# First expert stage writes its tiles to pair order by indirect writes, and the second attention loads them by plain transfers

## The chip, the core and the metric

The kernel runs on one core of a Trainium2 chip, as one launch. The time is the device time of that core in microseconds, the median over executions. The core's engines are PE (TensorE), DVE (VectorE), ACT (ScalarE), POOL (GpSimd) and SP (SyncE); PEld is PE's load of stationary operands. They run their own instruction streams and meet at semaphores.

## The reference

A decoder of four layers over x, 32 sequences of 128 rows with 128 columns, float32. Each layer adds a cross attention to a context of the same shape, then a mixture of experts with 8 experts. Rows are normed ahead of each.

```python
x = x + xattn0(ctx, norm(x));  x = x + ffn0(norm(x))   # each row goes to 2 of 8 experts (gelu, 512 wide)
x = x + xattn1(norm(x), ctx);  x = x + ffn1(norm(x))   # 2 of 8, gated, at most 256 slots an expert
x = x + xattn2(ctx, norm(x));  x = x + ffn2(norm(x))   # 2 of 8, gated
x = x + xattn3(norm(x), ctx);  x = x + ffn3(norm(x))   # 1 of 8 (gelu)
# ffn with two choices: out[row] = w0[row] * expert[e0[row]](row) + w1[row] * expert[e1[row]](row)
```

xattn1 is a linear attention with 16 heads of 8 columns: softmax over the columns of a head for queries and keys, keys times values summed over the context, queries times that sum, and a projection.

## The kernel before

The 4096 rows stay in SBUF as `x_rows`, 32 tiles of 128 rows, worked on in groups of four tiles. A stage ends with a barrier of all engines. The stages stand in this order: attention 0, router 0, experts 0, attention 1, router 1, experts 1, attention 2, experts 2, attention 3, experts 3, combine and store. Layers are counted from 0, so that "first expert stage" is `experts(0)` and "second attention" is `attention_1`.

**Router.** `route(layer, top, capacity)` sorts the (row, choice) pairs by expert. A slot is a place in that order, and a tile is 128 slots of one expert; layer 0 has 71 tiles (`TILES_TOP2`), layer 1 has 16. PE turns "which slot has this row" into "which row stands in this slot" by matmuls of one-hot halves: eight batches (`eight`), each of eight matmuls (line 1012) for layer 0, each after DVE has made its operands (lines 842 to 844) in one of two buffers. DVE then writes `source_rows` (line 921). For a layer in the list `SCATTERED`, eight more matmuls a batch (line 1016) mark whether the slot holds a pair and which choice, and DVE makes `pair_rows` of them (lines 923 to 932): for each slot the place of its pair, or a spare row of its own for an empty slot. For a layer not in it, DVE keeps `slots` instead (line 890): for each pair the slot it went to.

**Experts.** For each tile, in order: POOL gathers its 128 rows from `normed_rows_dram` by one indirect transfer (line 1152, 64 KB, buffer j modulo 8); PE turns it (line 1173); DVE copies the turned tile and the tile's expert weights into place (1255, 1257); PE multiplies (1183), ACT applies gelu (1217), PE multiplies again (1195), and DVE adds the bias (1249, semaphore `expert_kept`). PE's step k does turn k+2, first product k+1, second product k. For a layer outside `SCATTERED`, SP stores the tile in slot order (line 1136). For one in it, POOL writes the rows by an indirect transfer at `pair_rows` (line 1157), in the same loop and queue as the gathers: at step j it gathers tile j and then writes tile j - LAG, with LAG = 6. The gather of tile j waits only until PE has turned tile j - 8.

```python
for j in range(n_tiles + LAG):
    if j < n_tiles and not kept:
        if j >= SLOTS:
            pool.wait_ge(rows_turned.sem, ...)
        pool.indirect_dma_start(xr[:, j % SLOTS, :], None, xn, ...)
    i = j - LAG
    if scatters and i >= 0:
        pool.wait_ge(expert_kept.sem, ...)
        pool.indirect_dma_start(ys, ..., yo[:, i % SLOTS, :], None)
```

Layers 2 and 3 also write by line 1157, but there SP loads the tiles, so that POOL issues one indirect transfer a tile. Layer 1 issues both.

**Second attention.** It begins with a phase on the context alone: for each of eight groups PE projects keys and values (1550, 1569), DVE subtracts the maximum (1433, 1434), ACT exponentiates (1538), DVE scales (1448 to 1450), PE sums (1576) and DVE masks (1456, 1458). Between these, DVE adds the experts' rows to `x_rows`, weighted (`combine`, line 496), for groups 0 to 3 and takes their statistics; groups 4 to 7 follow in the second turn of the query phase. In the kernel before, POOL gathers those rows by 64 indirect transfers (line 1293, `gather_turns`), one for each tile and choice, and tells DVE by `rows_here`. The fourth attention (after layer 2) instead loads them by eight transfers of SP (`load_pairs`, line 1314, 512 KB each), since layer 2 writes in pair order. The code of DVE is written out by hand in its order; nothing is scheduled.

Of the kernel before, what the change touches and what calls it, by code (L numbers as in the profile page):

```python
# [31 lines left out]
MASKED = -1e30  # L32
FAR = 1.0e6
CAPACITY = 256
SCATTERED = (1, 2, 3)
KEPT = (2, 3)
REGION = B * P + P
SLOTS = 8
# [74 lines left out]
def build(nc, A, out):  # L113
    with ExitStack() as top:
# [147 lines left out]
        def flat(ap):  # L262
            return ap.rearrange("p a d -> p (a d)")
# [13 lines left out]
        with ExitStack() as ph:  # L277
            block = ph.enter_context(nc.Block())
# [193 lines left out]
        def combine_stream(dve, ch, i, w, layer):  # L472

            if layer in SCATTERED:
                dve.wait_ge(pairs_here[w].sem, i * 16 + (pairs_here[w].value + 16))
# [12 lines left out]
        def combine(dve, ch, g, layer):  # L488

            slots = CHOICES[layer]  # L490
            for k in range(slots):
                for j in range(G):
                    t = g * G + j
                    xt = flat(X[:, bass.ds(t, 1), :])
                    row = YY[:, bass.ds(t, 1), k, :] if layer in SCATTERED and slots == 2 else (XN, Y1)[k][:, bass.ds(t, 1), :]
                    ins = dve.scalar_tensor_tensor(xt, flat(row), WT[:, k, bass.ds(t, 1)], xt, ALU.mult, ALU.add)  # L496
# [276 lines left out]
        def route(layer, top, capacity):  # L773

            n_tiles = {0: TILES_TOP2, 1: TILES_CAP, 2: TILES_TOP2, 3: TILES_TOP1}[layer]
            with ExitStack() as ph:
# [56 lines left out]
                def _(dve):  # L833
# [48 lines left out]
                    if capacity:  # L882

                        ch.link(dve.tensor_tensor(posf[:, :, :], posf[:, :, :], keep[:, :, :], ALU.mult))
                        if layer not in SCATTERED:
                            dve.tensor_copy(POS[:, :, :], posf[:, :, :])
                        ch.link(dve.tensor_scalar(tmp[:, 0:2 * B // E, :].rearrange("p a e -> p (a e)"), keep[:, :, :].rearrange("p a b -> p (a b)"), -FAR, FAR, ALU.mult, ALU.add))
                        ch.link(dve.tensor_tensor(posf[:, :, :].rearrange("p a b -> p (a b)"), posf[:, :, :].rearrange("p a b -> p (a b)"), tmp[:, 0:2 * B // E, :].rearrange("p a e -> p (a e)"), ALU.add))
                    elif layer not in SCATTERED:
                        dve.tensor_copy(POS[:, 0:top, :], posf[:, 0:top, :])  # L890
# [30 lines left out]
                    dve.tensor_scalar(SOURCE[:, 0:n_tiles], found, float(HALF), None, ALU.add)  # L921
                    if layer in SCATTERED:
                        ch.link(dve.tensor_copy(pair_used[:, :], first))
# [44 lines left out]
                def _(pe):  # L968
# [39 lines left out]
                    def eight(i, s, first):  # L1008
                        pe.wait_ge(tiles_marked.sem, i + (marked0 + 1))
                        for r in range(EIGHT):  # L1010
                            own = bank[7][:, 0:n_tiles]
                            ins = pe.matmul(own, hot_row[:, s, :, r], row_at_tile[:, s, :, r], start=first and s == 0 and r == 0, stop=True, skip_group_check=True)
                            if layer in SCATTERED:
                                k = r % top
# [273 lines left out]
        def gather_group(pool, g, top):  # L1288

            for t in range(g * G, (g + 1) * G):  # L1290
                for k in range(top):
                    dst = (XN, Y1)[k]
                    pool.indirect_dma_start(dst[:, t, :], None, ys[0:TILES_TOP2 * P, :], bass.IndirectOffsetOnAxis(ap=POS[:, k, t:t + 1], axis=0)).then_inc(gathered[g % 2].sem, 16)

        def group_is_here(pool, g, top):
            pool.wait_ge(gathered[g % 2].sem, gathered[g % 2].value + 16 * G * top * (g // 2 + 1))
            pool.sem_inc(rows_here.sem, 1)
# [6 lines left out]
        def load_pairs(sp, layer):  # L1304

            top = CHOICES[layer]
            dst = YY if top == 2 else XN
            src = ys[0:top * B * P, :].rearrange("(t p k) d -> p t k d", p=P, k=2) if top == 2 else ys[0:B * P, :].rearrange("(t p) d -> p t d", p=P)
            for i in range(TURNS):
                for w in range(W):  # L1310
                    if i:
                        sp.wait_ge(pairs_here[w].sem, pairs_here[w].value + 16 * i)
                    at = slice((i * W + w) * G, (i * W + w + 1) * G)
                    sp.dma_start(dst[:, at], src[:, at]).then_inc(pairs_here[w].sem, 16)
# [58 lines left out]
        def gather_turns(pool, layer):  # L1373

            top = CHOICES[layer]
            for g in range(NG + 1):
                if g < NG:
                    gather_group(pool, g, top)
                if g >= 1:
                    group_is_here(pool, g - 1, top)  # L1380


        def attention_1(layer_before):
            assert layer_before not in SCATTERED
            with ExitStack() as ph:
                VX, KX = P + 16, P + 32
                FIRST = streams(pe=["kv_in", "kv"], act=["ctx_kept", "k_exp"], dve=["k_less", "v_scaled", "kv_masked"], tail=False)
# [16 lines left out]
                block = ph.enter_context(nc.Block())  # L1404
# [1 line left out]
                def first(g):  # L1406
                    return g // W, FIRST[g % W], T[g % W]

                @block.gpsimd
                def _(pool):  # L1410
                    gather_turns(pool, layer_before)

                @block.sync
                def _(sp):
                    sp.wait_ge(SS[W - 1].dve.sem, SS[W - 1].DVE.at(TURNS - 1, "u_normed"))
                    sp.dma_start(head_raw[:, 0:INNER], A["L2_xattn_Wq"]).then_inc(weights_x.sem, 16)
                    sp.dma_start(head_raw[:, INNER:3 * INNER], A["L2_xattn_Wkv"]).then_inc(weights_x.sem, 16)
                    sp.dma_start(head_o.rearrange("p (c d) -> p c d", d=P), A["L2_xattn_Wo"].rearrange("(c p) d -> p c d", p=P)).then_inc(weights_x.sem, 16)
# [966 lines left out]
        route(0, 2, 0)  # L2385
        experts(0)
        attention_1(0)
        route(1, 2, CAPACITY)
        experts(1)
# [26 lines left out]
```

## Time and profile before

| | us |
|---|---|
| median of 3 runs (1900.53 to 1907.52) | 1901.37 |
| the profiled execution's own time | 1909.33 |
| its span, first to last instruction | 1907.6 |
| PE busy | 1488.1 (78%) |
| DVE busy | 1164.3 (61%) |
| ACT busy | 824.9 (43%) |
| POOL busy | 763.8 (40%) |
| mean granted TensorE clock | 0.852 |

The shares are means over stages with different limits, so the stage is what is read: experts 0 from 186 to 341 us, the second attention from 343.6 to 596, experts 1 from 623.9 to 676. A wait in the profile is named by what ended it; "remote" means that the semaphore rose just then, but that no instruction of the profile ended near that moment, and "issue" that nothing shown was waited for.

### The profile page before, as it was taken

What the parts mean: (1) busy time and instruction counts of PE and PEld (TensorE: products, weight loads), DVE (VectorE), ACT (ScalarE), POOL (GpSimd) and SP (SyncE); (2) the same over time, 40 slices, a digit from 0 to 9 for tenths busy, and PEclk for the clock granted to TensorE, in tenths of its full rate; (3) what the DMA queues carried; (4) which work ended last, traced back from release to release, by engine and by line L of the source; (5) the groups of instructions that cost most, each with busy time, mean ns of one, the idle gap of its engine ahead of it and who ended that gap; (6) DMA issues with size and microseconds to landing.
All of it is one profiled execution on the core that took longest, in us unless ns stands there. A gap on an engine that the chain in (4) does not pass through costs nothing. (4 is left out here: it accounts for less than half of the span.)

```text
span 1907.6 us, 36653 instructions
## 1 busy us (share of the span) xinstructions
PE 1488.1 (78%) x10440; PEld 1337.0 (70%) x10441; DVE 1164.3 (61%) x3672; ACT 824.9 (43%) x2537; POOL 763.8 (40%) x757
## 2 busy tenths in 40 slices
PE   6776999425677639999999999999994898446394
PEld 4555899313466539999999999999993787224294
DVE  4556344217867337787778777777775455574244
ACT  4343455201222126666666666666661232313152
POOL 2011543560000535454747474756454355011442
PEclk8786899756666769999999999999997899766597
DMA  9002322110011230000000000000001522200223
GB/s 190 1 0 70 118 65 59 47 48 1 1 45 45 57 97 13 1 12 1 24 1 22 0 22 1 21 0 11 3 10 34 149 72 65 89 9 14 63 64 114
DMA packets 91845, 79.06 MB, mean 41 GB/s; under 512 B 16820, under 2 KB 78871, under 8 KB 91623
## 3 DMA queue, kind: packets, MB, share of 16 engines
q1 hardware_dynamic: 70712, 44.92, 9.0%
q0 software_dynamic: 11936, 24.52, 4.4%
q10 hardware_dynamic: 9104, 8.53, 1.5%
q8 instruction: 41, 0.67, 0.1%
q14 instruction: 52, 0.43, 0.1%
HBM read 51.36 MB, written 27.60 MB: 41 GB/s over the span
## 5 line engine op out<-in xcount | busy, mean ns | idle before, releaser
L1838 POOL TENSOR_TENSOR paired_rows<-paired_rows,rinv 128x1024 f32<-128x1024 f32 x128 | 242.3, 1893 | 284.6 <-DVE rinv L2123 281.6
L2002 ACT ACTIVATE paired_rows<-psum_banks,neg_max 128x256 f32<-128x256 f32 x512 | 237.4, 490 | 0.2
L2114 DVE TENSOR_TENSOR probs_turned_lo<-psum_banks,probs_turned_hi 128x512 fp32r<-128x512 f32 x256 | 175.5, 686 | 96.4 <-ACT probs_turned_hi L1984 82.8
L1888 PE MATMUL psum_banks<-y_turned_parts,queries_hi 128*128 128x256 f32 x1024 | 199.9, 293 | 3.0 <-DVEq L1739 3.0
L1923 PE MATMUL psum_banks<-probs_turned_hi,y_rows 128*128 128x512 f32 x512 | 192.0, 416 | 0.4 <-issue 0.4
L1984 ACT CAST probs_turned_hi<-psum_banks 128x512 fp32r<-128x512 f32 x256 | 151.1, 590 | 57.5 <-PE psum_banks L1872 55.1
L1872 PE MATMUL psum_banks<-ident,paired_rows 128*128 128x128 f32 x1024 | 154.9, 274 | 7.8 <-DVEq L1739 4.4
L1888 PEld LDWEIGHTS psum_banks<-y_turned_parts,queries_hi 128*128 128x128 f32 x1024 | 158.0, 191 | 3.5 <-issue 3.5
L2128 DVE TENSOR_REDUCE neg_max<-psum_banks 128x4 f32<-128x1024 f32 x128 | 155.9, 1218 | 6.5 <-PE psum_banks L1888 3.5
L1984 ACT CAST queries_hi<-psum_banks 128x512 fp32r<-128x512 f32 x128 | 75.0, 586 | 172.5 <-PE psum_banks L1911 167.6
L1888 PE MATMUL psum_banks<-y_turned_parts,queries_lo 128*128 128x256 f32 x512 | 144.5, 282 | 0.0
L1935 PEld LDWEIGHTS psum_banks<-expert_w_a,paired_rows 128*128 128x128 f32 x1024 | 133.8, 191 | 11.2 <-DVE paired_rows L2138 0.8
L1911 PE MATMUL psum_banks<-expert_w_b,expert_w_a 128*128 (+1 forms) x1024 | 138.6, 279 | 3.5 <-ACT tail_turned L1974 1.8
L1935 PE MATMUL psum_banks<-expert_w_a,paired_rows 128*128 128x128 f32 x1024 | 134.7, 274 | 0.6 <-issue 0.6
L1911 PEld LDWEIGHTS psum_banks<-expert_w_b,expert_w_a 128*128 128x128 f32 x1024 | 126.2, 193 | 7.4 <-ACT tail_turned L1974 3.2
L1872 PEld LDWEIGHTS psum_banks<-ident,paired_rows 128*128 128x128 f32 x1024 | 119.6, 142 | 10.6 <-DVEq L1739 5.1
L2114 DVE TENSOR_TENSOR queries_lo<-psum_banks,queries_hi 128x512 fp32r<-128x512 f32 x128 | 88.4, 690 | 43.6 <-ACT queries_hi L1984 34.8
L2002 ACT ACTIVATION_READ_ACCUMULATOR paired_rows<-psum_banks,neg_max 128x1 f32 x512 | 113.6, 222 | 0.0
L1217 ACT ACTIVATE hidden<-psum_banks,tile_w 128x128 f32<-128x128 f32 x284 | 81.2, 368 | 71.7 <-PE psum_banks L1183 52.1
L1923 PEld LDWEIGHTS psum_banks<-probs_turned_hi,y_rows 128*128 128x128 f32 x512 | 96.3, 188 | 17.9 <-issue 0.5
L1152 POOL DMA_INDIRECT tile_rows<-normed_rows_dram,source_rows x71 | 67.3, 948 | 93.5 <-PE psum_banks L1173 65.4
L1923 PE MATMUL psum_banks<-probs_turned_lo,y_rows 128*128 128x512 f32 x256 | 100.2, 391 | 0.0
(717 smaller groups left out, 3386.2 us busy)
## 6 DMA issues: line engine op xcount, KB each, us to landing
tile_rows__<-rows_by_expert SPq DMA_DIRECT2D x71, 64.5 KB
expert_rows<-expert_rows_sb SPq DMA_DIRECT2D x71, 64.0 KB, 1.5
normed_rows_dram<-paired_rows SPq DMA_DIRECT2D x2, 2048.0 KB, 8.9
staged_pairs<-expert_rows SPq DMA_DIRECT2D x8, 512.0 KB
paired_rows<-expert_rows SPq DMA_DIRECT2D x8, 512.0 KB, 6.0
tile_rows___<-rows_by_expert SPq DMA_DIRECT2D x39, 64.5 KB
x_rows<-in_x_dram SPq DMA_DIRECT2D x8, 256.0 KB, 5.3
expert_w_b<-in_L_ffn_w_dram SPq DMA_DIRECT2D x1, 2048.0 KB
```

What stands on the lines that cost most here:

```text
L1152: pool.indirect_dma_start(xr[:, j % SLOTS, :], None, xn, bass.IndirectOffsetOnAxis(ap=SOURCE[:, j:j + 1], axis=0)).then_inc(sorted_in[j % ...
L1217: ins = act.activation(hidT[:, s % 2, c * P:(c + 1) * P], hidden_bank(s, c // 2)[:, c % 2 * P:(c % 2 + 1) * P], ACT.Gelu, bias=w1[:, s % 4 ...
L1838: ins = pool.tensor_tensor(probs[:, p, :, :], probs[:, p, :, :], rinv[:, p, :].unsqueeze(2).to_broadcast([P, 4, 256]), ALU.mult)
L1872: ins = pe.transpose(bank[T_BANK][:, h * P:(h + 1) * P], probs[:, par, h, c * P:(c + 1) * P], ident[:, :])
L1888: ins = pe.matmul(bank[S_BANKS[par] + h // 2][:, (h % 2) * 256:(h % 2 + 1) * 256], queries[q][:, h, :], yparts[:, 2 * s2 + y, :], start=(k ...
L1911: ins = pe.matmul(bank[Q_BANK][:, h * P:(h + 1) * P], wqk[:, 4 * u3 + h, :], flat(KVT[:, bass.ds(b3, 1), P:2 * P]), start=True, stop=True)
L1923: ins = pe.matmul(bank[Z_BANK][:, :], yrows[:, 2 * s1 + y, k * P:(k + 1) * P], probsT[p][:, (u + 1) % 2, k, :], start=(k == 0 and n == 0), ...
L1935: ins = pe.matmul(bank[Y_BANK][:, 0:P], mixed[:, par, h, :], wvo[:, 4 * u0 + h, :], start=(u0 == 0 and h == 0), stop=(u0 == 3 and h == 3), ...
L1984: ins = act.copy(dst, bank[bank_][:, :])
L2002: ins = act.activation(probs[:, par, h, :], bank[S_BANKS[par] + h // 2][:, (h % 2) * 256:(h % 2 + 1) * 256], ACT.Exp, bias=nmax[:, par, h: ...
L2114: ins = dve.tensor_tensor(lo, bank[bank_][:, :], hi.bitcast(F32), ALU.subtract)
L2128: ins = dve.tensor_reduce(nmax[:, par, :], ps[:, S_BANKS[par]:S_BANKS[par] + 2, :].rearrange("p r (h k) -> p (r h) k", k=256), AX.X, ALU.m ...
```

## The change

Layer 0 joins `SCATTERED`, and the second attention takes its rows by `load_pairs`:

```diff
-SCATTERED = (1, 2, 3)
+SCATTERED = (0, 1, 2, 3)
...
         def attention_1(layer_before):
-            assert layer_before not in SCATTERED
+            assert layer_before in SCATTERED
...
-                @block.gpsimd
-                def _(pool):
-                    gather_turns(pool, layer_before)
-
                 @block.sync
                 def _(sp):
+                    load_pairs(sp, layer_before)
                     sp.wait_ge(SS[W - 1].dve.sem, SS[W - 1].DVE.at(TURNS - 1, "u_normed"))
```

Four things follow from the first line. Router 0 gets line 1016 on PE and lines 923 to 932 on DVE, and loses line 890. In experts 0, POOL writes tiles by line 1157, and SP's 71 stores go. DVE's combine of layer 0 reads both choices of a row side by side. Arithmetic is unchanged.

On PE in router 0, each batch of eight matmuls becomes one of sixteen; before the change and after it a batch begins so:

```order
-L1012 MATMUL psum_banks<-row_at_tile,hot_slot_row 128x71 x16
+L1012 MATMUL psum_banks<-row_at_tile,hot_slot_row 128x71
+L1016 MATMUL psum_banks<-hot_tile,hot_slot_row 128x71
+L1012 MATMUL psum_banks<-row_at_tile,hot_slot_row 128x71
+L1016 MATMUL psum_banks<-hot_tile,hot_slot_row 128x71
```

The second kind stands between the first ones, with a weight load of its own each.

On POOL, from experts 0 into the second attention (`expert_kept` is DVE's line 1249, `rows_turned` is PE's line 1173):

```order
-L1152 DMA tile_rows<-normed_rows_dram,source_rows 128x128 x8
-L1152 DMA tile_rows<-normed_rows_dram,source_rows 128x128 [waits rows_turned] x63
-L1047 UNCONDITIONAL_BRANCH
-L1409 UNCONDITIONAL_BRANCH [waits barrier_Pool_Activation_PE_DVE_SP_gather]
-L1293 DMA paired_rows<-expert_rows,slots 128x128 x16
...
+L1152 DMA tile_rows<-normed_rows_dram,source_rows 128x128 x7
+L1157 DMA expert_rows<-expert_rows_sb,pair_rows 17280x128 [waits expert_kept]
+L1152 DMA tile_rows<-normed_rows_dram,source_rows 128x128
+L1157 DMA expert_rows<-expert_rows_sb,pair_rows 17280x128 [waits expert_kept]
+L1152 DMA tile_rows<-normed_rows_dram,source_rows 128x128 [waits rows_turned]
```

From the eighth gather on, each gather stands behind a write that waits for a finished tile, seven tiles back; seven writes follow the last gather. The 64 gathers of line 1293 are gone.

On SP the stores go and the loads come (the rows between are the same pair for tile after tile):

```order
-L1136 ISA [waits expert_kept]
-L1136 DMA expert_rows<-expert_rows_sb 128x128
...
+L1314 DMA paired_rows<-expert_rows 128x4x256 x4
+L1314 DMA paired_rows<-expert_rows 128x4x256 [waits pairs_here0]
+L1314 DMA paired_rows<-expert_rows 128x4x256 [waits pairs_here1]
+L1314 DMA paired_rows<-expert_rows 128x4x256 [waits pairs_here2]
+L1314 DMA paired_rows<-expert_rows 128x4x256 [waits pairs_here3]
```

The first four loads stand at the head of the second attention with no wait; each later one waits only for the landing of its forerunner.

## Rows read from the trace of the kernel before

**Rows 1.** Waits, 200 to 341 us (us in total, times, longest).

```profile
POOL tile_rows L1152 <- PE psum_banks L1173: 65.4, 60, 1.9
```

**Rows 2.** Instructions of lines 1152 and 1173 (ns min/median/max, first and last start).

```profile
L1152 POOL DMA_INDIRECT tile_rows<-normed_rows_dram,source_rows x71: 938/942/1209, 186.0 to 320.8; - x71
...
L1173 PE MATMUL psum_banks<-ident,tile_rows x71: 272/273/477, 193.3 to 335.8; 128*128 128x128 f32 x71
```

**Rows 3.** Timeline, first expert stage and its end: start, length, instruction, [idle before].

```profile
201.35 0.29 DVE L1249 TENSOR_TENSOR expert_rows_sb<-psum_banks,expert_b 128x128 f32<-128x128 f32 x1 [3.77 <-PE psum_banks L1195]
...
341.03 0.29 DVE L1249 TENSOR_TENSOR expert_rows_sb<-psum_banks,expert_b 128x128 f32<-128x128 f32 x1 [0.96 <-PE psum_banks L1195]
...
343.63 0.62 ACT L1527 COPY u_rows<-ctx_turned 128x512 f32<-128x512 f32 x1 [4.16 <-PEq L1047]
```

**Rows 4.** Timeline, second expert stage: POOL's reads and writes in turn, and two rows of PE.

```profile
638.34 1.01 POOL L1157 DMA_INDIRECT expert_rows<-expert_rows_sb_,pair_rows  x1 [5.96 <-ACT expert_rows_sb_ L1223]
...
642.23 0.96 POOL L1152 DMA_INDIRECT tile_rows_<-normed_rows_dram,source_rows  x1 [0.30 <-PE psum_banks L1173]
...
645.15 0.27 PE L1173 MATMUL psum_banks<-ident,tile_rows_ 128*128 128x128 f32 x1
...
653.42 0.98 POOL L1157 DMA_INDIRECT expert_rows<-expert_rows_sb_,pair_rows  x1 [2.54 <-ACT expert_rows_sb_ L1223]
...
664.14 0.98 POOL L1157 DMA_INDIRECT expert_rows<-expert_rows_sb_,pair_rows  x1 [0.76 <-issue]
```

**Rows 5.** Timeline, second expert stage: a late release, then its last write and the next stage.

```profile
645.85 1.16 PE L1183 MATMUL psum_banks<-tile_turned_,expert_w_b 128*128 128x128 f32 x8 [0.43 <-issue]
...
649.81 0.42 DVE L1262 TENSOR_TENSOR hidden_<-psum_banks,gate_ 128x256 f32<-128x256 f32 x1 [4.01 <-remote]
...
675.87 0.96 POOL L1157 DMA_INDIRECT expert_rows<-expert_rows_sb_,pair_rows  x1 [0.31 <-issue]
...
681.29 0.38 SPq L1704 DMA_DIRECT2D staged_pairs<-expert_rows  x1
```

**Rows 6.** Instructions of line 1293, then the timeline of the second attention's start.

```profile
L1293 POOL DMA_INDIRECT paired_rows<-expert_rows,slots x64: 940/944/953, 344.3 to 423.0; - x64
...
345.26 3.78 PE L1569 MATMUL psum_banks<-wsmall,u_rows 128*128 128x256 f32 x8
...
360.80 1.14 PE L1576 MATMUL psum_banks<-expert_w_a 128*128 128x144 f32 x8
...
397.67 0.69 DVE L1433 TENSOR_REDUCE head_sums___<-psum_banks 128x64 f32<-128x512 f32 x1 [37.12 <-remote]
...
420.06 0.61 DVE L1456 TENSOR_TENSOR expert_w_a<-psum_banks,head_blocks 128x432 f32<-128x432 f32 x1 [16.25 <-remote]
...
433.36 0.61 DVE L1456 TENSOR_TENSOR expert_w_a<-psum_banks,head_blocks 128x432 f32<-128x432 f32 x1 [12.48 <-remote]
...
467.42 1.12 DVE L450 TENSOR_SCALAR u_rows<-x_rows,mean_var__,rstd__ 128x128 f32<-128x128 f32 x4
```

**Rows 7.** Transfers (KB each, median us to landing).

```profile
paired_rows<-expert_rows SPq DMA_DIRECT2D x8, 512.0 KB, 6.0
```

**Rows 8.** Fourth attention: instructions of line 2257 and a wait of DVE.

```profile
L2257 POOL DMA_INDIRECT rows_by_expert<-paired_rows,top_experts x32: 965/969/1009, 1708.7 to 1788.0; - x32
...
1729.76 0.69 DVE L2336 TENSOR_REDUCE neg_max<-psum_banks 128x4 f32<-128x512 f32 x1 [13.07 <-remote]
```

**Rows 9.** Timeline, first router: the last batch of eight on PE, DVE's line 921 after it.

```profile
182.04 1.26 PE L1012 MATMUL psum_banks<-row_at_tile,hot_slot_row 128*128 128x71 f16 x8 [0.31 <-DVE row_at_tile L844]
...
184.77 0.23 DVE L921 TENSOR_SCALAR source_rows<-psum_banks 128x71 uint32<-128x71 f32 x1
```

**Rows 10.** Timeline, second router: first and last of DVE's eight steps on pairs.

```profile
621.45 0.16 DVE L923 COPY pair_used_<-psum_banks 128x16 f32<-128x16 f32 x1
...
622.85 0.17 DVE L932 TENSOR_TENSOR pair_rows<-pair_found_,pair_spare_ 128x16 uint32<-128x16 f32 x1
```

**Rows 11.** Instructions of line 1257 (ns min/median/max, first and last start).

```profile
L1257 DVE COPY tile_w<-expert_w_a x71: 417/419/491, 194.1 to 337.0; 128x516 f32 x71
```

## The prediction

> **What bounds the kernel now.** I read the waits of each stage first, then the timeline where one stage hands over to the next, then every place where POOL issues indirect transfers. The page's table alone misleads: PE is 78% busy as a mean, but the change touches two stages that lie apart. In the first expert stage PE is the bound. POOL's 71 gathers wait for PE's turns, 65.4 us in 60 waits [rows 1], and PE turns 71 tiles from 193.3 to 335.8 us, 2.04 us a tile [rows 2]. In the second attention nothing is busy. POOL issues 64 gathers from 344.3 to 424 us, one each 1.25 us (the last starts at 423.0, so 78.7/63), and DVE stands still three times, 37.12, 16.25 and 12.48 us, released by "remote" [rows 6]. The middle of these waits is the strangest: the reader should see that the matmuls which the releases belong to (line 1569 and, from 360.80, line 1576) stand in the timeline as started before 362 us, while DVE's waiting instructions start at 397.67 and 420.06. So PE's release comes up to 58 us after its matmuls as recorded.
>
> That late release has company. In the fourth attention POOL issues 16 indirect writes from 1708.7 us, and DVE waits 13.07 us for a "remote" release [rows 8]. In the second expert stage, POOL's gathers and writes alternate without a gap, PE's line 1183 is recorded at 645.85 for 1.16 us, and DVE's instruction behind it starts at 649.81 [rows 5]. All these stand inside or just behind 10 or more indirect transfers in a row. I take it that a dense row of POOL's transfers holds PE's releases back; the trace does not say how.
>
> **The change part by part.** All differences are taken in the profiled execution (1909.33 us, 8.0 us over the median of the runs shown) and added to the median, 1901.37.
>
> *Router 0.* PE gets 64 matmuls more. A batch of eight takes 1.26 us, so one follows another each 0.136 us if the last takes 0.31, an estimate [rows 9]. Sixteen need 2.2 us, and with a hand-over about 2.25. Then PE sets the pace instead of DVE: eight batches take 18.0 us instead of 12.6 (from 170.7 to 182.04 + 1.26), 5.4 us later. DVE's line 921 starts at 184.77 [rows 9], 1.5 us after PE's last batch, because it has other work first; that hides 1.2, and 4.2 stay. DVE's eight steps more cost 1.6 us, from 621.45 to 623.02 in the second router [rows 10]; the dropped line 890 is one short cast, counted as 0. Sum +5.8. The low end is 1.6, where PE keeps up at its upper clock level.
>
> *Experts 0.* POOL's row becomes gather, write, gather, write. One indirect gather costs 0.942 us [rows 2] and a write 0.98 to 1.01, with 0.30 between; a pair in the second expert stage is 2.57 us (638.34 to 640.91 by that sum). PE needs 2.04 a tile, so POOL becomes the bound. Write 0 needs tile 0, whose bias add starts at 201.35 and takes 0.29 [rows 3]: write 0 starts at 201.9. From it to write 64, the first behind the last gather, stand 64 pairs. Then come six more writes at 1.28 us, 7.7 us; tile 70's gather, 1.3 us ahead of write 64, lands in 2.9 (642.23 to 645.15 [rows 4], line 1173 after line 1152) and needs 5.5 from turn to bias add (335.8 to 341.3 [rows 2, 3]), which is 7.1 and fits. From the issue of the last write to the next stage are 5.4 us in the second expert stage (675.87 to 681.29 [rows 5]) and I take 5.8. So the second attention starts at 201.9 + 64p + 13.5 instead of 343.6 [rows 3].
>
> The size of p decides. Its lower end is 2.57, a POOL that never waits: +36.3 us. The nearest row that has everything is the second expert stage: write 0 at 638.34 and write 9 at 664.14 are nine pairs apart, 2.87 us a pair, since POOL waited 2.54 us once for tiles that PE's late release had delayed [rows 4]. That gives +55.5. Layer 0 is heavier, 2.04 us a tile on PE, against 12 matmuls where it has 16, and PE's clock falls after a wait of some us, so each late release costs more. I take p = 2.95: 64 x 2.95 = 188.8, the next stage at 404.2, +60.6. The upper end: a wait of 3.5 us each 15 us and another 2.5 us at the lower clock leave 9 us of work in 15, 4.6 tiles, p = 3.25, +79.8. SP's 71 stores and DVE's waits for them are gone; SP was not waited for, so that is worth nothing but the 2.3 us of the last landing, which is in the difference above.
>
> What is queued behind the new wait: gather j stands behind write j-7. PE's second product of tile k stands behind the turn of tile k+2, so tile k is finished about 5.6 us after gather k+2 was issued (2.9 to land, 2.7 of work, an estimate), and its write comes six and a half pairs, 16.7 us, after gather k; gather k+2 is two pairs, 5.1 us, behind gather k. That leaves 16.7 - 5.1 - 2.9 - 2.7 = 6 us in which PE may be late without POOL noticing. Beyond it POOL waits, and PE's loads come later by as much.
>
> *Second attention.* 64 gathers go from POOL. SP issues four loads of 512 KB at once, 6.0 us to landing each in the fourth attention [rows 7]; the first is wanted 24 us after the stage's start even without the stalls (434 - 65.9 - 343.6), so they are hidden. If the three stalls go, 37.12 + 16.25 + 12.48 = 65.9 us come free. Late next is PE: its projections take about 1 us (line 1550, between the first gather and 345.26) and 3.78 us a group at the lower clock [rows 6], the sums 2 x 1.14, eight groups 57 us, while the phase without stalls is 467.42 - 65.9 - 343.6 = 57.9 long [rows 6]. PE and DVE would be near level, so I take off 4 us: -62. Bounds: -66, and 0 if the stalls have another cause.
>
> Sum: +5.8 + 60.6 - 62 = +4.4 us, 1901.4 + 4.4 = 1906, rounded. A measurement of this kernel tells about 0.5% (9.5 us) from no change, so the forecast is no change that can be told.
>
> **A rule weighed.** The copies of line 1257 (71 of 0.419 us, SBUF to SBUF [rows 11]) run while POOL issues gathers in this stage, and those gathers last 942 ns at the median against 944 for line 1293, where no such copy runs [rows 2, 6]. The Trainium skill, "SBUF — State Buffer", section "SBUF: two separate sides", says that a VectorE copy between SBUF places in its two-port mode locks GpSimd out of the port by which it writes the descriptors of its own transfers. By that rule, with POOL as the bound, each copy would lengthen a transfer; this trace shows no such length, so the sum goes without it.
>
> **The rivals.**
> - *POOL never waits (27%).* PE's late releases stay within the 6 us. For it: its pace of 2.57 asks PE for 79% of its time only, and in experts 0 of before, with one transfer each 2.04 us, POOL waits 1.9 us at most [rows 1]. Against it: the same pair pattern did make POOL wait in the second expert stage [rows 4]. Then +5.8 + 36.3 - 62 = -19.9: 1881.
> - *A vicious circle of late releases (26%), slower.* It sits in experts 0: the row of transfers is dense for over 160 us, and dense rows gave delays of up to 37.12 us [rows 6]. From a delay of 6 us on, POOL stops, PE recovers at its lower clock, and it begins again. At p = 3.25: +5.8 + 79.8 - 62 = +23.6, 1925. If each round is 12 us of issue, 6 us of reserve and 12 us of standstill for 7 tiles, p = 4.3: +91, 1992. Against it: when POOL stopped in the second expert stage, PE's releases came at once.
> - *The stalls stay (6%).* If DVE's three waits have a cause of their own, +66, 1968. Against: they begin and end with the gathers.
> - *The copies lock POOL out (3%).* 71 x 0.42 = 30 us on top of the forecast: 1936.
>
> **How the numbers follow.** The forecast's case (38%) is p from 2.75 to 3.15, which is 1894 to 1919. Faster by over 0.5% (below 1892) needs the first rival, nearly whole, and the lowest edge of the forecast's case: 29%. Within 0.5%: 31%, nearly all of it the forecast's case. Slower: 40%, the upper part of the forecast's case and the other rivals. The forecast's own range is 1894 to 1919. The range for 8 in 10 goes from 1880, the first rival, to 1950, which leaves out the far end of the circle and the stalls that stay, about 17%.
>
> **What would show it.** In the profile after: the start of line 1157's row and its last start, divided by tiles, gives p (2.57, 2.95 or over 3.2); POOL's idle time before line 1157 by DVE's line 1249 shows how often it waited; "remote" among DVE's and ACT's waits in that stage shows the late releases. The second attention's context phase should last 58 to 65 us instead of 124, with no "remote" of over 5 us. Line 1012 and line 1016 should start from 170.7 to about 188.5. The forecast is wrong if the context phase still has its stalls, or if p lies outside 2.75 to 3.15.

## The result and the profile after

The changed kernel takes 1925.74 us (median of 4 runs, 1924.32 to 1925.94), the kernel before 1902.43 in the same comparison (4 runs): ratio 1.0104, 95% interval 1.0077 to 1.0130, so +19.8 us by the ratio (+14.6 to +24.7), +23.3 by the medians. Slower, and clear of noise. The profiled execution has a span of 1924.2 us, 16.6 more than that of before, which was itself 8 us over its median.

I read the handover rows first, as they split the change into its terms. Instructions of the changed kernel (ns min/median/max, first and last start):

```profile
L1152 POOL DMA_INDIRECT tile_rows<-normed_rows_dram,source_rows x71: 942/969/1205, 193.5 to 409.5; - x71
L1157 POOL DMA_INDIRECT expert_rows<-expert_rows_sb,pair_rows x71: 968/991/1233, 207.7 to 421.8; - x71
```

The first instruction of its second attention, and the first row behind the context phase (timeline):

```profile
428.28 0.62 ACT L1524 COPY u_rows<-ctx_turned 128x512 f32<-128x512 f32 x1 [8.67 <-PEq L1047]
...
486.49 1.11 DVE L450 TENSOR_SCALAR u_rows<-x_rows,mean_var__,rstd__ 128x128 f32<-128x128 f32 x4
```

Against [rows 2, 3, 6]: the first gather starts at 193.5 instead of 186.0 (+7.5, router 0 with all ahead of it); from there to the second attention 234.8 us instead of 157.6 (+77.2); its context phase lasts 58.2 us instead of 123.8 (-65.6). Everything behind it is 2.5 us shorter. That is +16.6, the difference of the two spans. The +23.3 of the medians is 6.7 us more, since the profiled execution of before (1909.33) took longer than any of its four runs; no row places these 6.7 us.

In the first expert stage POOL is the bound, but not an always busy one. Waits, 193 to 428 us (in total, times, longest):

```profile
POOL expert_rows L1157 <- DVE expert_rows_sb L1249: 53.7, 34, 5.5
...
POOL tile_rows L1152 <- PE psum_banks L1173: 1.5, 5, 0.3
...
DVE expert_rows_sb L1249 <- PE psum_banks L1195: 56.9, 39, 3.1
DVE expert_rows_sb L1249 <- remote: 48.8, 16, 3.7
```

The 65.4 us in which gathers waited for PE's turns [rows 1] are down to 1.5 us. In their place writes wait 53.7 us for finished tiles, and of the waits of the bias add that finishes them (line 1249) 48.8 us are "remote". One such wait, in the timeline around 248 us:

```profile
243.71 1.15 PE L1195 MATMUL psum_banks<-expert_w_a,hidden 128*128 x8
...
244.99 0.99 POOL L1157 DMA_INDIRECT expert_rows<-expert_rows_sb,pair_rows  x1 [0.30 <-issue]
...
245.81 0.39 PE L1183 MATMUL psum_banks<-tile_turned,tile_w 128*128 128x128 f32 x2
246.28 0.97 POOL L1152 DMA_INDIRECT tile_rows<-normed_rows_dram,source_rows  x1 [0.30 <-issue]
248.27 1.66 ACT L1217 ACTIVATE hidden<-psum_banks,tile_w 128x128 f32<-128x128 f32 x6 [2.94 <-remote]
248.47 0.29 DVE L1249 TENSOR_TENSOR expert_rows_sb<-psum_banks,expert_b 128x128 f32<-128x128 f32 x1 [3.54 <-remote]
...
249.03 1.15 PE L1195 MATMUL psum_banks<-expert_w_a,hidden 128*128 x8 [2.83 <-ACT hidden L1217]
249.04 1.00 POOL L1157 DMA_INDIRECT expert_rows<-expert_rows_sb,pair_rows  x1 [1.79 <-DVE expert_rows_sb L1249]
```

PE's matmuls of line 1183 end at 246.20. POOL's row of transfers ends at 247.25, and ACT, waiting for those matmuls, starts at 248.27, one microsecond after POOL has stopped. DVE starts at 248.47, 3.6 us after the end of its matmuls (line 1195, 243.71 + 1.15). ACT's and DVE's own releases go out without such a delay (POOL starts 0.6 us after DVE's row at 248.47). All three stand still, then the next burst begins. The pattern repeats: between 233 and 296 us bursts of four and of six transfers, ten in 15.8 us, later bursts of two, four and six. From the first write to the last gather POOL stops 28 times for more than 0.6 us; in 25 of them DVE's next bias add starts 0.78 to 1.44 us after POOL's last transfer has ended.

The pace: write 0 starts at 207.67, the last gather at 409.48 and write 64, the first behind it, at 410.76. That is p = 203.09 / 64 = 3.17 us a pair. The expectations of e6 and e7 name 3.21, which counts one write too far. The six writes that follow wait for the last tiles and take 11.0 us.

```profile
207.67 1.01 POOL L1157 DMA_INDIRECT expert_rows<-expert_rows_sb,pair_rows  x1 [5.50 <-DVE expert_rows_sb L1249]
...
409.48 0.97 POOL L1152 DMA_INDIRECT tile_rows<-normed_rows_dram,source_rows  x1 [0.31 <-issue]
410.76 1.07 POOL L1157 DMA_INDIRECT expert_rows<-expert_rows_sb,pair_rows  x1 [0.30 <-issue]
```

### The profile page after: what moved, and what is told of

Its sections match the earlier page's. It is cut to its first block and busy times, and to the rows that moved or that the text cites. A ratio compares the mean times of both kernels' runs of the same rounds, so it can differ in the third digit from the quotient of the medians.

```text
span 1924.2 us, 36527 instructions
## 1 busy us (share of the span) xinstructions
PE 1511.5 (79%) x10504; PEld 1356.2 (70%) x10505; DVE 1164.9 (61%) x3679; ACT 827.3 (43%) x2537; POOL 778.2 (40%) x764
## 5 line engine op out<-in xcount | busy, mean ns | idle before, releaser
L1195 PE MATMUL psum_banks<-expert_w_a,hidden 128*128 x568 | 88.4, 305 | 31.8 <-ACT hidden L1217 27.7
L1195 PEld LDWEIGHTS psum_banks<-expert_w_a,hidden 128*128 128x128 f32 x568 | 77.9, 212 | 36.6 <-issue 35.6
```

The source lines that it names most:

```text
L1195: ins = pe.matmul(out_[:, 0:P], hidT[:, u % 2, c * P:(c + 1) * P], W2[:, bass.ds(off + c * P, P)], start=(c == 0), stop=(c == NC - 1))
```

## The experiments

All comparisons are with the kernel before on the same chip. That turned out to matter: these runs fell on four chips, and on them the kernel before takes 1906 (e1 to e4) and 1908 us (e11, e12), but 1807 (e5 to e8) and 1803 us (e9, e10).

### e1: router 0 alone

```diff
+BY_PAIR = (0, 1, 2, 3)       # SCATTERED stays (1, 2, 3)
-                    if layer in SCATTERED:
+                    if layer in BY_PAIR:            # DVE's steps for pair_rows
-                            if layer in SCATTERED:
+                            if layer in BY_PAIR:    # line 1016
```

> The kernel before, with only router 0 making the pair tables (64 more matmuls, eight more steps of DVE, line 890 kept); nothing reads them. The prediction's term says +5.8 us over the kernel before. Rival: PE keeps up with DVE at its upper clock level and only DVE's steps remain, +1.6. In the profile the batches should last 18 us if PE sets the pace, 12.6 if DVE does.

Measured: ratio 1.0032 [1.0020, 1.0044], +6.1 us (+3.8 to +8.4). PE's batches are no longer apart; DVE waits for the last matmul of the batch before last (timeline, line numbers one higher):

```profile
183.44 0.45 DVE L843 TENSOR_TENSOR hot_tile<-iota_tile_by_eights,slot_tile_half 128x568 f16<-128x568 f16 x1 [0.48 <-PE psum_banks L1017]
...
185.56 0.46 DVE L843 TENSOR_TENSOR hot_tile<-iota_tile_by_eights,slot_tile_half 128x568 f16<-128x568 f16 x1 [0.47 <-PE psum_banks L1017]
...
190.01 0.23 DVE L922 TENSOR_SCALAR source_rows<-psum_banks 128x71 uint32<-128x71 f32 x1
```

A batch each 2.12 us, at PE's pace. The term +5.8 stands, and the rival of +1.6 lies outside the interval.

### e2 and e4: the second attention without indirect gathers

```diff
# e2: experts 0 as before (SP stores in slot order), loads of the change
-                    gather_turns(pool, layer_before)
+                    load_pairs(sp, layer_before)
# e4: as many transfers of POOL, of the same size, plain ones
-  pool.indirect_dma_start(dst[:, t, :], None, ys[...], bass.IndirectOffsetOnAxis(ap=POS[:, k, t:t + 1], axis=0))
+  pool.dma_start(dst[:, t, :], ys[(2 * t + k) * P:(2 * t + k + 1) * P, :])
```

> The kernel before (tiles of layer 0 stored in slot order by SP, no pair tables), but the second attention takes its rows by the eight plain transfers of SP instead of 64 gathers of POOL. It leaves out the order of layer 0's expert rows. Theory (dense POOL transfers hold PE's releases back): the context phase is 58 to 66 us instead of 124, no remote wait over 5 us, -62 us: 1840. Rival (the stalls have a cause of their own in this stage): they stay, 1902. With the change at +23, the first expert stage and the router would then cost +85 by the theory, +23 by the rival.

> The kernel before, with the 64 gathers of the second attention replaced by 64 plain transfers of 64 KB that POOL issues just as densely. It leaves out the choice of rows. If any dense row of POOL's transfers holds releases back, the remote stalls stay within 10 us of the 66 us before: 1890 to 1905. If it takes the indirect kind, they go: 1840 to 1850.

Measured: e2 1840.41 us against 1905.82, ratio 0.9664 [0.9640, 0.9688], -64 us. e4 1843.89, ratio 0.9673 [0.9657, 0.9690], -62 us. Neither has a remote wait in this stage, and DVE has none under "issue" in the context phase. In e2 the context phase goes from 341.56 to 399.80 us, 58.2 long, as in the changed kernel. e4's transfers (instructions), and the start and end of its context phase (timeline):

```profile
L1293 POOL DMA_DIRECT2D paired_rows<-expert_rows x64: 552/650/747, 343.7 to 376.9; - x64
```

```profile
343.15 0.62 ACT L1527 COPY u_rows<-ctx_turned 128x512 f32<-128x512 f32 x1 [4.08 <-PEq L1047]
...
401.48 1.11 DVE L450 TENSOR_SCALAR u_rows<-x_rows,mean_var__,rstd__ 128x128 f32<-128x128 f32 x4
```

One plain transfer each 0.53 us is more than twice as dense as [rows 6] and holds nothing back. So the wording "a dense row of POOL's transfers" in the prediction was too wide: on this chip it takes the indirect kind. The rival "the stalls stay" has fallen. Both runs leave out which rows are combined; the number and the size of the transfers are kept in e4.

### e3: a long pause after each gather

```diff
+                    pool.drain()
+                    pool.memset(SPACER[-1][:, :], 0.0)    # spare tile, 128x512
```

> The kernel before, with POOL draining and filling a spare 128x512 tile after each of the 64 gathers of the second attention, so that gathers start each 1.9 to 2.2 us instead of 1.25. Theory (releases wait for a row of transfers without a pause): the stalls shrink to single waits of about 2 us, the context phase goes to 65 to 80 us (groups 0 to 3 need 32 gathers, 61 to 70 us), 1845 to 1860. Rival (it is the number of transfers in flight, not POOL's pauses): the same number of transfers gives the same lateness, 1895 to 1910. Rival (own cause): 1902.

Measured: 1964.61 us, ratio 1.0304 [1.0288, 1.0320], +58: my number missed on the other side. No remote wait is left in the stage, so the theory's half holds. But the drain lasts 1.7 us beside the fill's 0.53, gathers start each 3.35 us instead of the 1.9 to 2.2 I had written, and DVE waits for rows instead, so that the context phase lasts 139.0 us (347.65 to 486.66) and not 65 to 80 (waits, 340 to 600 us):

```profile
DVE x_rows L496 <- POOLq L1303: 123.5, 7, 28.4
POOL spacer L1299 <- issue: 108.8, 64, 2.1
```

### e5 and e10: a short pause after each gather

```diff
+                    pool.wait_ge(spaced.sem, spaced.value)   # the fill before is done: no wait
+                    spaced.value += 1
+                    pool.memset(SPACER[-1][:, :], 0.0).then_inc(spaced.sem, 1)
```

> The kernel before, with POOL filling a spare 128x512 tile after each of the 64 gathers, without the drain of e3 (there 1.7 us a gather went into it). Gathers start each 1.8 us (0.95 + 0.53 and two gaps of 0.16 to 0.3). Theory (a row of indirect transfers without a pause holds PE's releases back; a pause each 1.3 us frees them): no remote wait over 2.5 us in the second attention, groups 0 to 3 are there after 58 to 62 us, 1842 to 1860. Rival (the pauses of e3 were long enough, 2.4 us; 0.8 us is too short to let a release through): remote waits of over 5 us stay, 1880 to 1905.

> The kernel of e5 again (a fill of 128x512 on POOL after each gather of the second attention). On a chip with late releases: no remote wait over 2.5 us in that stage, 50 to 60 us less than the kernel before (1842 to 1856). If 0.8 us is too short a pause there: remote waits stay and it gains under 20 us. On a chip without them: +10 to +20 us as in e5, since gathers for groups 0 to 3 then come later.

Measured: e5 1821.75 against 1807.40, ratio 1.0086 [1.0061, 1.0112]; e10 1820.72 against 1802.86, ratio 1.0096 [1.0067, 1.0126]. The "theory" number of e5 (1842 to 1860) was made for a kernel before of 1902 and says nothing here, where there was nothing to free. Gathers start each 1.67 us, the context phase of e10 lasts 70.9 us (342.94 to 413.81), and groups 0 to 3 come late for DVE (waits of e10, 343 to 480 us):

```profile
DVE x_rows L496 <- POOLq L1304: 14.1, 4, 8.8
```

That is most of the price of +15.5 and +17 us, as I read it: no trace of the kernel before was taken on these chips.

### e6 and e7: the distance between gather and write

```diff
-            LAG = 6
+            LAG = 7 if layer == 0 else 6      # e6; 4 in e7
```

> The changed kernel with writes seven tiles behind the gathers in the first expert stage instead of six. If POOL waits because PE's lateness eats a reserve of 6 us, one tile more of reserve (2.6 us) makes POOL wait less: p from 3.21 to 2.9 to 3.1, 1905 to 1918. Theory (releases come only when POOL pauses, so a pause is made whatever the reserve is): the bursts get longer and the waits longer, p stays within 0.08 of 3.21, 1920 to 1931.

> The changed kernel with writes four tiles behind. By the reserve: p over 3.4, 1940 to 1960. By the pauses alone: shorter bursts, more and shorter waits, and p near 3.2, 1918 to 1932; below 3.1 if short bursts hold releases back less.

The changed kernel with another distance. Measured, both on a chip without late releases: 1850.43 us (ratio 1.0239) and 1857.88 (1.0284) against 1807.40. From the first gather to the second attention 193.6 us (194.2 to 387.83) with a distance of seven, 200.9 (193.3 to 394.23) with four; the distance of six took 196.1 in e9 on another such chip. The waits for finished tiles are few in both (5.8 us and 12.6 us). A longer distance is worth 2 us or so there; whether the reserve matters where releases come late is not tested by these two. Their expected numbers were made for a kernel before of 1902 us and cannot be compared.

### e8: writes without gathers

```diff
-  pool.indirect_dma_start(xr[:, j % SLOTS, :], None, xn, ...)            # layer 0
+  sp.dma_start(xr[:, j % SLOTS, :], xn[j % B * P:(j % B + 1) * P, :])
```

> The changed kernel with the 71 gathers of the first expert stage replaced by 71 plain loads of SP of the same size; POOL's 71 indirect writes stay. It leaves out the choice of rows. Theory (the price is two indirect transfers a tile in one row on POOL): POOL issues one each 2.04 us, PE is the bound again, no remote wait over 2.5 us, the stage lasts 150 to 155 us instead of 235, 1840 to 1852. Rival (the writes to scattered rows are themselves slow to land or hold PE): the stage stays above 200 us, over 1890.

The changed kernel, without the choice of rows. Measured: 1823.26 us against 1807.40, ratio 1.0103 [1.0042, 1.0164], and 27 us under e6 on the same chip; its second attention starts at 360.83 us, 27.0 before e6's.

```profile
L1161 POOL DMA_INDIRECT expert_rows<-expert_rows_sb,pair_rows x71: 957/997/1225, 212.8 to 352.1; - x71
```

A write each 1.99 us (139.3/70): PE is the bound again, near the 2.04 us of [rows 2]. Here scattered writes alone did not slow PE; the cost came with the second indirect transfer a tile on one engine. The expected 1840 to 1852 was again made for the other kind of chip.

### e9: the change itself on another chip

> The changed kernel once more, beside the kernel before on the same chip. The chip of e5 to e8 (before: 1807 us) showed no late release in any of its four traces; the chips of the first comparison and of e1 to e4 did (before: 1902 and 1906). On a chip with late releases: p 3.1 to 3.3, +18 to +28 us. On a chip without them: p = 2.4 to 2.6 and nothing to win in the second attention, +5.8 + 36 = +38 to +48 us over a kernel before of about 1807. Rival (the difference of chips is only their clock): p and the remote waits as in the first trace on either chip.

Measured: 1853.04 us against 1802.86, ratio 1.0271 [1.0228, 1.0315], +50 us (+41 to +57). The same program, word for word, 73 us faster than on the first chip, and yet a worse change. Instructions and waits of e9:

```profile
L1157 POOL DMA_INDIRECT expert_rows<-expert_rows_sb,pair_rows x71: 965/989/1238, 207.7 to 383.1; - x71
```

```profile
POOL expert_rows L1157 <- DVE expert_rows_sb L1249: 8.2, 7, 5.5
```

Up to the first write both traces agree within 0.1 us. Then POOL does not wait in e9 before its last gather (5.5 of the 8.2 us are the wait for tile 0, the rest lies behind the last gather); write 0 at 207.74, the first write behind the last gather at 374.61, p = 2.61. No remote wait stands in the stage. The context phase is 389.64 to 448.74, 59.1 us. Mean granted clock of the first expert stage 0.96 against 0.89 (windows: stretch, length, busy time of PE, PEld, DVE, ACT and POOL, granted clock, DMA share, GB/s):

```profile
193.00:428.00 235.00, 167.91 (x1207) 156.73 (x1207) 65.78 (x213) 83.63 (x285) 141.33 (x142) 0.89 0.17 56
```

```profile
193.00:389.00 196.00, 163.48 (x1207) 146.76 (x1207) 66.09 (x213) 82.42 (x285) 141.53 (x142) 0.96 0.22 67
```

The first row is the changed kernel on the first chip, the second e9. PE's work is the same, and it is busy for 167.9 and 163.5 us: of the 39 us that the first row is longer, 4.4 are slower work and the rest is standstill. So the rival "the chips differ only in their clock" is out.

Nor is this stage longer on the first chip whatever runs in it. The trace of e10, from the chip of e9, has the first expert stage of the kernel before (instructions, timeline):

```profile
L1152 POOL DMA_INDIRECT tile_rows<-normed_rows_dram,source_rows x71: 940/942/1238, 187.4 to 319.6; - x71
...
342.94 0.62 ACT L1535 COPY u_rows<-ctx_turned 128x512 f32<-128x512 f32 x1 [4.69 <-PEq L1047]
```

From the first gather to the second attention that is 155.5 us, against 157.6 on the first chip. With the change it is 196.1 (389.64 - 193.50) against 234.8. In this stage the two chips part only when POOL issues two indirect transfers a tile.

### e11 and e12: a pause after every second gather, and the kernel before

```diff
+                    if (2 * t + k) % 2 == 1:     # else as in e5
```

> The kernel before, with POOL filling a spare 128x512 tile after every second gather of the second attention (0.54 us; without a fill gathers start each 1.25 us, with one after each 1.66 us). Gathers then start each 1.45 us on average, groups 0 to 3 are there after 47 us instead of 53. On a chip with late releases: if a fill between every two gathers frees the releases, 50 to 62 us less than the kernel before; if it takes a longer pause, remote waits of over 5 us stay in the stage and it gains under 30 us. On a chip without them: +3 to +12 us, less than e5's +15.6, since DVE's waits for rows (14.1 us in e10) are the price.

> The kernel before itself, for its trace on this chip. On a chip where it takes about 1805 us: no remote wait over 5 us in the second attention, its context phase about 60 us instead of 124, and the same first expert stage as on the first chip. On a chip where it takes about 1903: the stalls of 37, 16 and 12 us again, near the same places.

Measured: e11 1850.40 us against 1907.92, ratio 0.9706 [0.9687, 0.9724], -56 us. It computes everything that the kernel before does, and is the fastest such version measured on a chip with late releases, 75 us under the changed kernel's 1925.7 of another comparison. e12, on the same chip, took 1912.59. Three stalls of the same lengths as in [rows 6] stand in its timeline:

```profile
346.60 0.62 ACT L1527 COPY u_rows<-ctx_turned 128x512 f32<-128x512 f32 x1 [4.59 <-PEq L1047]
...
400.78 0.69 DVE L1433 TENSOR_REDUCE head_sums___<-psum_banks 128x64 f32<-128x512 f32 x1 [37.26 <-issue]
423.24 0.61 DVE L1456 TENSOR_TENSOR expert_w_a<-psum_banks,head_blocks 128x432 f32<-128x432 f32 x1 [16.30 <-issue]
436.54 0.61 DVE L1456 TENSOR_TENSOR expert_w_a<-psum_banks,head_blocks 128x432 f32<-128x432 f32 x1 [12.48 <-remote]
...
470.61 1.11 DVE L450 TENSOR_SCALAR u_rows<-x_rows,mean_var__,rstd__ 128x128 f32<-128x128 f32 x4
```

Two of them are now put down to "issue" instead of "remote": the label of a wait whose end the profile cannot place is not to be trusted, its length is. That is why the lengths of the context phase carry the argument. And e11 (timeline):

```profile
346.35 0.62 ACT L1535 COPY u_rows<-ctx_turned 128x512 f32<-128x512 f32 x1 [4.50 <-PEq L1047]
...
347.03 0.94 POOL L1295 DMA_INDIRECT paired_rows<-expert_rows,slots  x1 [22.92 <-POOLq L1047]
348.27 0.94 POOL L1295 DMA_INDIRECT paired_rows<-expert_rows,slots  x1 [0.30 <-issue]
349.22 0.54 POOL L1300 MEMSET spacer<- 128x512 f32 x1
349.92 0.95 POOL L1295 DMA_INDIRECT paired_rows<-expert_rows,slots  x1 [0.17 <-issue]
...
407.87 1.12 DVE L450 TENSOR_SCALAR u_rows<-x_rows,mean_var__,rstd__ 128x128 f32<-128x128 f32 x4
```

The context phase is 61.5 us instead of 124.0 on the same chip, 62.5 less, without a remote wait; DVE has none under "issue" there either. Its 64 gathers take longer (347.0 to 439.3, one each 1.47 us) but that lies beside other work. A fill of 0.54 us after every second gather is enough. It also stretches the row from 1.25 to 1.47 us a gather; whether the pause or the pace does it was not separated. The rival that counts transfers (e3's expectation) is out, since their number is the same 64.

## Why the prediction was right or wrong

The forecast was 1906 and no change that can be told; it is 1925.7 and slower. That is outside the forecast's own range (1894 to 1919) and inside the range for 8 in 10 (1880 to 1950); p = 3.17 lies 0.02 above the forecast's case of 2.75 to 3.15, so by its own sign the forecast is wrong. By its steps:

- *Router 0, +5.8.* Right: +6.1 in e1, with PE setting the pace. In the traces the first gather is 7.5 us later, 1.7 more than the term.
- *Experts 0.* The form of the term was right, the size of p was too small. 201.9 + 64p + 13.5 with the measured p = 3.17 gives 418.5, or +74.9 over 343.6; measured are +77.2 from the first gather on. I took p = 2.95 for the likeliest and so +60.6. Of the 16.6 us that were missing, 14.3 are p. The rest is the ends: from write 64 to the second attention 17.5 us instead of 13.5 (the six last writes take 11.0 instead of 7.7), and write 0 comes 14.2 us after the first gather instead of 15.9. The failing step is the one that scaled the second expert stage's 2.87 by "layer 0 is heavier": nine pairs in which POOL stopped once say little on a stage of 64. Between 233 and 296 us the stage runs in a cycle of ten transfers in 15.8 us, of which 12.9 us (10 x 1.29, half of p = 2.57) are issue and 2.9 standstill. My upper end for p, "a wait of 3.5 us each 15 us and another 2.5 us at the lower clock", gave 3.25 and 1925. The kind of thing the second rival (26%) tells is what happened, POOL stopping again and again for late tiles, but in stops of 2 us and not from a delay of 6 us on, and its far end (p = 4.3) did not come. What I set against it, that releases come at once when POOL stops, holds to about one microsecond and did not prevent it. That its 1925 is also the measured time is partly luck: with p = 3.17 its sum is +18.7, or 1920.
- *The 6 us of reserve.* Wrong as a bound. In the timeline above two releases come 2.1 and 3.6 us late, no remote wait is longer than 5.7 us, and POOL waited all the same, 27 times between write 1 and the last gather. A reserve hides a single late release. Here several a cycle hit the turn, the two products and the bias add in turn, PE falls behind POOL at each, and the reserve is used up once and not won back. That is my reading of the rows; no run took the reserve alone on such a chip.
- *Second attention, -62.* Right: -65.6 by the traces, -64 in e2. The stalls go with the indirect gathers (e2, e4) and with pauses between them (e3, e11). PE's level with DVE cost less than the 4 us taken off: the phase lasts 58.2 us, against 57.9 without the stalls. But the argument that the stalls "begin and end with the gathers" was a wrong reading of [rows 6]. Two of them end in the middle of the row (397.67 and 420.06), while POOL goes on without a pause, and the third at 433.36, 9.5 us after the last gather has ended (422.96 + 0.94). Gathers of before around the first:

```profile
396.74 0.95 POOL L1293 DMA_INDIRECT paired_rows<-expert_rows,slots  x1 [0.30 <-issue]
398.00 0.94 POOL L1293 DMA_INDIRECT paired_rows<-expert_rows,slots  x1 [0.30 <-issue]
```

- *Copies that lock POOL out (3%).* The gathers last 969 ns at the median here against 942 in [rows 2], 27 ns and not the 419 of a copy. Gathers of the second expert stage, which alternate with writes in the kernel before too, have 968. The writes do show something: in the changed kernel those that begin during a copy of line 1257 last up to 1.23 us, and the median of all is 0.99 (timeline):

```profile
242.13 0.42 DVE L1257 COPY tile_w<-expert_w_a 128x516 f32 x1
242.25 1.16 POOL L1157 DMA_INDIRECT expert_rows<-expert_rows_sb,pair_rows  x1 [0.30 <-issue]
```

With a mean of 1.02 us over 71 writes that is 2 to 3 us in all, an estimate. The rival with its 30 us is out, as the forecast had it.

- *POOL never waits (27%).* Wrong on the first chip, right on e9's: p = 2.61 against 2.57. But its other half, the 62 us of the second attention, is then missing, so the sum is +5.8 + 36.3 = +42 and not -20, and +50 [+41, +57] was measured. In the traces of that chip the stage is 40.6 us longer than in e10 (196.1 and 155.5). The two cases were tied to each other, and I had set their chances as if they were apart: the releases that hold POOL up in experts 0 are the same ones whose end is the gain in the second attention.

The explanation, with what carries it: on some chips, indirect transfers that POOL issues one after another hold back the releases of PE's matmuls (e2, e3, e4 and e11 for the second attention). In the first expert stage the releases come about one microsecond after POOL stops (25 of 28 stops); in the long row of before they also came without a stop, after tens of microseconds. The change takes 64 indirect transfers out of the second attention, which gives back 65.6 us, and makes the first expert stage's 71 into 142 in one row. There a pair of 2.57 us stands against PE's 2.04 a tile, with what the forecast put at the ends of the row +36.3 us. The late releases add 64 x (3.17 - 2.57) = 38 us, and the ends 2 more. The same program without late releases is 38.7 us shorter in this stage (e9).

Open: what in the chip holds the releases back, what ends a late release where POOL does not stop, and why it happens on some chips only. In experts 0 no run removed the late releases on a chip that has them: e8, where the transfers are thinned, ran on a chip that has none. There is no trace of the kernel before on such a chip; that its second attention has no stalls there is inferred from its time, 1803 to 1807 us, and from e5 and e10.

## What to carry to other kernels

Count the indirect transfers per tile on POOL before giving it another one: at 1.29 us each, two a tile make a floor of 2.57 us. If a semaphore of PE comes late beside a row of POOL's indirect transfers, a pause of half a microsecond on POOL after every second one may give back nearly all of it (e11, -56 us). Where there was nothing to give back, a pause after every one cost 15 to 17 us (e5, e10); one after every second was not measured there. Put two cases of one mechanism into one case when setting chances, and take no stage's steady pace from a stage with a dozen tiles.

## What the hardware showed that I had not expected

- Chips of one kind differ by 5% on this kernel: before 1902 to 1908 us in three comparisons, 1803 and 1807 in two others. The difference is not a clock that is lower throughout. With the changed kernel, 38.7 of the 72 us stand in the first expert stage, and the third one, with a single indirect write a tile, goes from 126.0 us (1508.6 to 1634.6) to 107.5 (1463.5 to 1571.0) from first to last write, at a granted clock of 1.00 on both. No remote wait stands there; ACT's longest wait for line 1183 is 2.3 us on the one and 1.4 on the other. What makes these 18.5 us was not tested.
- POOL's indirect transfers, one each 1.25 us, hold PE's releases back, and DVE stood still for up to 37.1 us; 64 plain ones of the same size, one each 0.53 us, do not (e4).
- The stalls are regular: 37.1, 16.2, 12.5 us in one trace of before, 37.3, 16.3, 12.5 on a chip of another comparison.
- A drain on POOL behind an indirect gather lasts 1.7 us (e3).
